# Which PSUM banks the score tiles and the small transposes of an attention stage take in turn

## The reference, cut to what matters

```
q = x @ Wq + bq;  k = x @ Wk + bk;  v = x @ Wv + bv
scores = einsum('bqd,bkd->bqk', q, k) / sqrt(hd)
scores = where(causal, scores, -inf)
weights = softmax(scores, axis=-1)
out = einsum('bqk,bkd->bqd', weights, v)
return out @ Wo + bo
```

## Time and profile before

| what | us |
|---|---|
| median of 3 runs | 1505.39 |
| the profiled execution | 1504.49 |
| its span on the core | 1502.4 |
| PE busy | 1433.5 |
| DVE busy | 972.2 |
| ACT busy | 775.7 |
| POOL busy | 314.9 |

### The profile page before, as it was taken

One profiled execution on the slowest core, in us unless ns is written; L12 is line 12 of the kernel. 1 busy time (PEld: TensorE's weight loads), 2 busy tenths in 40 slices (PEclk: granted clock), 3 DMA queues, 4 the chain that ended last, 5 costly groups with the idle time before them and its releaser, 6 DMA issues. The chain is left out here.

```text
span 1502.4 us, 24878 instructions
## 1 busy us (share of the span) xinstructions
PE 1433.5 (95%) x10064; PEld 1045.0 (70%) x10064; DVE 972.2 (65%) x1862; ACT 775.7 (52%) x1098; POOL 314.9 (21%) x199
## 2 busy tenths in 40 slices
PE   8999999999999999898999999998888999899998
PEld 6677777777777776444555555556767788788886
DVE  3355545454645467797778778784667676667665
ACT  4433333333423335678867877864446565643333
POOL 0021212111212124000000000003246576640001
PEclk9999999999999999999999999999999999999999
DMA  7203030313121251001101101000301100021112
GB/s 273 82 28 111 27 111 28 111 31 107 56 83 27 89 187 39 22 0 57 56 2 56 57 17 40 1 17 26 97 29 57 57 29 1 1 79 62 56 57 84
DMA packets 48131, 88.38 MB, mean 59 GB/s; under 512 B 7201, under 2 KB 15009, under 8 KB 46610
## 3 DMA queue, kind: packets, MB, share of 16 engines
q1 hardware_dynamic: 48018, 86.80, 16.9%
HBM read 57.43 MB, written 29.36 MB: 58 GB/s over the span
## 5 line engine op out<-in xcount | busy, mean ns | idle before, releaser
L1004 PE MATMUL psum<-early,high 128*128 128x512 fp8e4 x1024 | 233.4, 379 | 5.9 <-DVE low_r L976 4.1
L1004 PEld LDWEIGHTS psum<-early,high 128*128 128x128 fp8e4 x1024 | 97.7, 98 | 124.1 <-DVE low_r L976 5.5
L411 POOL TENSOR_TENSOR rms<-ms,mhalf 128x16 f32<-128x16 f32 x30 | 88.4, 2946 | 342.4 <-DVE ms L474 342.4
L126 PE MATMUL psum<-Qh_r,Kh 128*128 128x512 f32 (+1 forms) x272 | 112.0, 412 | 17.6 <-ACT high L1410 6.5
L1011 PE MATMUL psum<-high,b_act 128*128 128x512 fp8e4 x512 | 115.4, 379 | 1.3 <-DVE Ql_r L981 0.8
L126 PE MATMUL psum<-early_r,high_r 128*128 128x512 f32 x256 | 106.6, 417 | 5.8 <-DVE early_r L437 5.8
L1484 DVE TENSOR_TENSOR c_gm<-psum,c_gm 128x512 f32<-128x512 f32 (+2 forms) x136 | 87.1, 640 | 28.9 <-PE psum L128 12.3
L128 PE MATMUL psum<-Qh_r,Kl 128*128 128x512 f32 (+1 forms) x272 | 104.9, 386 | 0.0
L127 PE MATMUL psum<-Ql_r,Kh 128*128 128x512 f32 (+1 forms) x272 | 104.8, 385 | 0.0
L580 ACT ACTIVATE early<-psum 128x512 f32<-128x512 f32 x64 | 38.3, 598 | 122.3 <-PE psum L128 117.2
L128 PE MATMUL psum<-early_r,low_r 128*128 128x512 f32 x256 | 101.4, 396 | 0.0
(11 more groups left out here) (288 smaller groups left out, 3432.7 us busy)
## 6 DMA issues: line engine op xcount, KB each, us to landing
low<-x_dram SPq DMA_DIRECT2D x9, 1024.0 KB, 5.6
wst<-in_L_ffn_w_gating SPq DMA_DIRECT2D x16, 512.0 KB, 4.7
xs<-in_L_attn_x SPq DMA_DIRECT2D x8, 1024.0 KB, 7.4
high<-x_dram SPq DMA_DIRECT2D x8, 1024.0 KB, 8.1
xt<-in_x_turned SPq DMA_DIRECT2D x7, 1024.0 KB, 4.8
x_dram<-xs SPq DMA_DIRECT2D x7, 1024.0 KB, 4.9
x_dram<-low SPq DMA_DIRECT2D x5, 1024.0 KB, 4.3
wst<-in_L_ffn_w_linear SPq DMA_DIRECT2D x16, 256.0 KB, 4.5
```

The lines of the kernel that those rows point to most:

```text
L126: tensor.matmul(out, hi_w, hi_x, start=first, stop=False, skip_group_check=True)
L411: nc.gpsimd.tensor_tensor(rms_of(b, c), ms_of(b, c), const["mhalf"][:, 0:H], ALU.pow).then_inc(*done)
L1004: last = t.matmul(out[:, h, :], w8g[:, tile + k, (2 * m + h) * P:(2 * m + h + 1) * P], x8[:, u, k, :], start=k == 0, stop=k == DC - 1)
```

## The change

Score tiles of blocks 2 to 7 take four banks in turn, 0, 1, 2 and 7. The transposes of the maxima, the broadcasts, the transposed heads and the outputs take two, 3 and 4. Every score tile of these blocks then waits for the copy of the tile four places back, and every small job for the reader of the small job two places back, where it was three. The exceptions stay as they were. No instruction is added, removed or moved on any engine.

```diff
         if kind == "r":
-            w, n_r = (4, 5)[n_r % 2] if n_r < 4 else n_r % (2 if i < 2 else 3), n_r + 1
+            w, n_r = (4, 5)[n_r % 2] if n_r < 4 else (n_r % 2 if i < 2 else (0, 1, 2, 7)[n_r % 4]), n_r + 1
             uses[name] = copied(*name[1:])
...
             elif kind == "oT" and i >= NB - 2:
                 w = 7
             else:
-                w, n_m = (3, 4, 7)[n_m % 3], n_m + 1
+                w, n_m = (3, 4)[n_m % 2], n_m + 1
```

## The result

The changed kernel takes 1493.26 us, the median of 6 runs (1492.56 to 1498.20), against 1505.12 for the kernel before in 6 runs: ratio 0.9929, 95% interval 0.9910 to 0.9949. The forecast was 1495.2 us with a range of 1487.0 to 1501.5, and faster was its likeliest sign. The profiled execution took 1492.56 us, its span 1490.5.

A forecast was written before the change was run, and what follows sets the result against it. TensorE was taken to bound the kernel, with idle time ahead of score tiles to win. Terms of 10.9 us less a 1.65 us half-clock charge gave 9.25 us: 1504.49 to 1495.2 us, range 1487.0 to 1501.5.

The forecast's parts named there:

- The cause of the waits: Ahead of score tiles, 1062 to 1300 us: 13 waits, 15.06 us in all, end with the copy three tiles back.
- The small jobs at nothing: Transposes, broadcasts, heads and outputs on two banks: price 0, at most 1.5 us over three tight places.
- The slower rival: Outputs wait for the reader two back and score tiles queue behind: 5.2 us slower, 1509.7 us, chance 0.06.
- the term of `r(5,19)`: Block 5's 2.98 us wait moves one tile on; one score tile's time is won, 1.2 us.
- the others: Gains at the other score waits of blocks 2 to 7: 0.4, 3.2, 1.6, 0.8, 0.7, 1.0, 0.9 and 1.1 us.
- the number in its bracket: The length of a wait ahead of a score tile in the trace before, such as 1.59 or 0.98 us.
- the step: Blocks 3 to 4: removing waits of 1.92, 1.24 and 0.79 us wins 3.2 of 3.95 us.
- the transfer rival: The load of `low` lands at its old time; earlier lead is lost, 4.2 us stay, 1500.3 us, chance 0.17.
- The charge for a new half-clock stretch: Longer TensorE waits before `r(4,0)` and `pv(3,0)`, some 2 us each, may bring one such stretch: 1.65 us charged.
- Nothing is won: TensorE finds the next wait in each score wait's place, as exponentials and maxima set the pace: 1504.5 us, chance 0.09.

The follow-up runs named there:

- the first profile: Profiled execution of the changed kernel, unaltered, from its first timing: 1492.56 us; the median of those 6 runs was 1493.26 us.
- the second: Profiled execution of the changed kernel, unaltered, timed once more beside other kernels: 1497.16 us; the median of that timing was 1496.3 us.
- The two careless seams: Against the kernel before, four score banks in blocks 2 and 3 alone (1502.86 us) or from block 4 on alone (1498.47 us), before the turn's start was mended.

## Why the prediction was right, point by point

**The cause of the waits: right.** With three score banks all 13 are there, with four, under either set of bank numbers, they go or move.

**The small jobs at nothing: right.** Ratio 1.0003 when they alone change. The slower rival needed a mean of 0.39 us at each output. Its waits appeared only with a single bank, in two places, and even then the time was 1495.57 us beside 1496.3 for the change.

**Term by term.** Without the term of `r(5,19)`, the others were 9.7 us and measured 13.1 up to `r(7,31)`. The error is one-sided, and much of it has one cause. I took a removed wait at the number in its bracket. The lead across each single removed wait grew by more: 1.59 gave 1.87 at `r(4,11)`, 0.98 gave 1.25, 0.76 gave 1.03, 1.02 gave 1.30, 0.57 gave 0.85 and 0.53 gave 0.81, each 0.27 or 0.28 us above its bracket. TensorE's timeline after shows what it is, at `r(4,11)`, which no longer waits:

```profile
1129.07 0.39 PE L128 MATMUL psum<-Qh_r,Kl 128*128 128x512 f32 x1
1129.30 0.39 PE L126 MATMUL psum<-Qh_r,Kh 128*128 128x512 f32 x1
1129.53 0.39 PE L127 MATMUL psum<-Ql_r,Kh 128*128 128x512 f32 x1
```

The matmul before the tile ends at 1129.46 (such ends are modelled by the profile), and the tile's first starts at 1129.30, 0.16 us before that: TensorE overlaps the end of one job with the start of the next. And its second follows the first after 0.23 us. Where the tile waited, in the trace before, the first took 0.50 us and the second followed after 0.34, 0.11 us more. A job that waits loses both, 0.16 + 0.11 = 0.27 us, on top of the idle time. In block 2 a half-clock stretch went as well (the lead is 1.0 behind `r(2,8)` and 1.3 ahead of `y(0,0)`), and the 2.04 us wait of `y(0,0)` for its input took that back (-0.71). Besides, waits too small for the list went as well: 0.08 us of idle time at `r(4,7)` and 0.06 at `r(6,7)`, where the lead grew by 0.33 and 0.30. At the turn to block 4, 1.24 became 1.61, as the step said ("most of the 1.24 falls into the same lead").

**The mis-sized term is that of `r(5,19)`: 1.2 against -0.2.** The step said that the wait moves one tile, which it did, and that GpSimd's addition and `c_var` "should shift together", which they didn't. The load of `low` was issued at 1168.82 in place of 1174.81, 6.0 us early: that is the lead from before the 0.76 us wait was removed. VectorE came to `c_var` 7.1 us early (1185.58 to 1178.46). So the two overlap by 1.0 us more, and `c_var` took 2.88 us in place of 1.86. Of the 1.4 us that the term lacks, this is the largest part. The part of the transfer rival that was right is this: a load keeps the lead of the work that issued it, and what is won after the issue can be lost where the load's reader and the faster engine meet. Its price was 1 us, not 5.

The Trainium skill, "SBUF — State Buffer", section "SBUF: two separate sides", says that the port pair which VectorE shares with GpSimd is under an exclusive lock for the whole instruction, where VectorE's step is in a two-port mode or has two SBUF inputs. The traces agree in that `c_var` ended with the addition in all eleven, within 0.04 us. That the meeting, and not the load, makes the wait is shown by the two kernels with the steps on GpSimd: 3.2 us won with three banks by the ratio, and with four a lead that grows by 3.4 us where the change alone lost 0.2. That it is the ports was not isolated: no run had the addition on other data, and none shows whether `c_var` is a step of the kind that the page names.

**The charge for a new half-clock stretch, 1.65: not due in the first profile, due in the other.** I had named two places, before `r(4,0)` and `pv(3,0)`, with "some 2 us" of waiting each. The waits came, 1.61 and 2.04 us. In the first execution neither was followed by a stretch at half clock, in the second both were, at 1113.6 and 1127.2. What decides it is not shown: the charge is right in one execution and not in the other. The forecast had one of two; without the charge it would have been 1493.6, which is nearer to the median of the six runs; from that of all ten, 1494.5, the two are about equally far.

**How much of the fit is luck.** In stage C the first profiled execution won 13.2 us, the second 6.5 (it entered 0.85 us ahead and ended 7.36 ahead). The forecast of 9.25 lies between. So the mechanism was right, but that the number came within 2 us of either median is partly luck: the terms were 2.3 us short of the first execution, and the half-clock stretches move a single execution by more than that.

**"Nothing is won": wrong, as said.** TensorE's waits for exponentials grew by 1.1 us (`c_rows`, 0.96 to 2.04), beside 15 us of score waits removed or moved. The Trainium skill's sentence on PSUM double-buffering ("TensorE: Matmul & The Clock Gate", section "HAM oscillation — how this bites in real kernels") doesn't carry over: here a fourth bank gave 11.9 us by the medians.

**What I said would show it.** Idle time ahead of line 126 between 1062 and 1290 under 6 us: wrong. It is 8.3, or 6.9 without block 1's tile, since `r(2,9)`, `r(4,0)` and `r(5,20)` alone have 6.2. The half-clock stretch near 1104 gone: right. VectorE's waits for TensorE smaller (11.1 to 7.2 us at the maxima) and that for `oh` unchanged: right. No wait above 0.5 us with line 1503 as its end: right. The last score tile about 9 us earlier: it is 11.7, and stage D kept its length. New half-clock stretches, named as a sign of being wrong: none in the first execution, where each of the three has a counterpart before, but four in the second that the first doesn't have.

## What to carry to other kernels

To judge one more buffer in a rotation, put the start of each waiting job beside the end of the last reader n and n + 1 places back; then count more than the bracket for a wait that goes entirely (some 0.27 us here), and ask of each whether the next engine later stood idle for the work behind it. And before a gain of a few us is explained, profile the same kernel twice. Where a rotation changes its length in the middle of a run, see to it that the first jobs of the new one still meet the oldest buffer. The two careless seams here made one tile wait 1.2 and 0.8 us more; mending them gave 1.9 us by the medians in one kernel, within the noise, and nothing in the other. A load keeps the lead that its issuer had, so look at where its reader meets an engine that has gained more.

## What was not expected of the hardware

A 128x4 step on VectorE took 2.88 us beside GpSimd's 4.55 us addition, 0.17 alone, while the statistics just before it, beside the same addition (1176.76 to 1181.31), ran in their usual 0.69:

```profile
1177.51 0.69 DVE L1507 BATCH_NORM_STATS2 c_bs<-high 128x6 f32<-128x512 f32 x1
```

Moved to GpSimd the step took 0.23 us in seven of eight blocks and 1.13 in the other, in which VectorE ran a subtraction of 1.2 us beside it, and the kernel was 3.7 us faster by the medians (1493.26 to 1489.53). And the number of half-clock stretches in one stage differed between executions of one program, three against six from 1062 us on, with 4.6 us between their times.
